# Field-pair tower on TensorE: sums of products in array tiles of 128 rows by 32 columns

## The reference

```python
z = jnp.sum(x, axis=-1)
xi = x[:, II, :]
xj = x[:, JJ, :]
outer = jnp.einsum('bpd,pde,bpe->bp', xi, kernels, xj)
h = jnp.concatenate([z, outer, dense_ctx], axis=1)
h = jnp.maximum(h @ W_top1 + b_top1, 0.0)      # 544 -> 512
h = jnp.maximum(h @ W_top2 + b_top2, 0.0)      # 512 -> 256
y = h @ W_top3                                 # 256 -> 1
```

## Time and profile before

| | |
|---|---|
| median of the runs | 843.35 us (843.25 to 846.5) |
| the profiled execution | 841.05 us, span 839.2 us |
| TensorE matmul (PE) | 804.7 us busy, 96% |
| VectorE (DVE) | 616.2 us, 73% |
| GpSimd (POOL), issuing gathers | 484.0 us, 58% |
| ScalarE (ACT) | 142.4 us, 17% |
| granted TensorE clock | 1.000 |

### The profile page before, as it was taken

One profiled execution on the slowest core, in us unless ns is written; L12 is line 12 of the kernel. 1 busy time (PEld: TensorE's weight loads), 2 busy tenths in 40 slices (PEclk: granted clock), 3 DMA queues, 4 the chain that ended last, 5 costly groups with the idle time before them and its releaser, 6 DMA issues.

```text
span 839.2 us, 33255 instructions
## 1 busy us (share of the span) xinstructions
PE 804.7 (96%) x15452; PEld 367.9 (44%) x15452; DVE 616.2 (73%) x613; ACT 142.4 (17%) x219; POOL 484.0 (58%) x518
## 2 busy tenths in 40 slices
PE   0699999999999999999999999999999999999998
PEld 0267767677754433333333333333333333333333
DVE  0477886588867788889855678988854588988850
ACT  0211022212120320120210320021111212011002
POOL 6777777777777777777777567767743340000000
PEclk9999999999999999999999999999999999999999
DMA  9611111111111111111111111111100010000000
GB/s 327 211 31 31 31 31 30 29 32 34 30 29 28 29 29 29 31 29 29 29 27 27 22 26 28 29 28 28 29 17 14 14 20 2 2 2 2 2 3 0
DMA packets 24387, 29.44 MB, mean 35 GB/s; under 512 B 13365, under 2 KB 13623, under 8 KB 24122
## 3 DMA queue, kind: packets, MB, share of 16 engines
q0 software_dynamic: 16384, 16.81, 10.2%
q1 hardware_dynamic: 7856, 10.49, 3.7%
q10 hardware_dynamic: 10, 0.01, 0.0%
HBM read 27.27 MB, written 0.01 MB: 33 GB/s over the span
## 4 chain that ended last, share of the span: by engine, by line
PE 93%; POOL 2%; DVE 2%; issue 1%; DMA 1%; ACT 0%; DVEq 0%; ACTq 0%
PE y L618 52%; PE accs L636 25%; PE y L598 4%; PE y L680 4%; PE y L668 3%; PE y L697 3%; POOL rows L371 2%; DVE prod L563 2%; PE y L673 1%; PE y L710 1%; DMA rows<-tbl,ids_sb 1%; PE y L649 0%; DMA ids_sb<-ids 0%; DVEq L265 0%; ACT h L484 0%
## 5 line engine op out<-in xcount | busy, mean ns | idle before, releaser
L563 DVE TENSOR_TENSOR prod<-y,xt 128x1024 f32<-128x1024 f32 (+1 forms) x525 | 576.4, 1157 | 170.9 <-PE y L618 167.5
L371 POOL DMA_INDIRECT rows<-tbl,ids_sb x512 | 483.3, 944 | 201.8 <-issue 125.1
L618 PE MATMUL y<-xt,kw 64*32 64x512 f32 (+1 forms) x9920 | 471.2, 509 | 5.6 <-DVE prod L563 2.2
L618 PEld LDWEIGHTS y<-xt,kw 64*32 64x32 f32 x9920 | 185.6, 107 | 245.3 <-issue 218.6
L636 PE MATMUL accs<-prod,ones_strip 64*32 64x512 f32 (+1 forms) x4960 | 242.6, 504 | 1.1 <-issue 0.6
L636 PEld LDWEIGHTS accs<-prod,ones_strip 64*32 64x32 f32 x4960 | 106.4, 107 | 110.3 <-issue 102.6
L417 ACT COPY xt<-y 128x1024 f32<-128x1024 f32 (+2 forms) x48 | 34.9, 728 | 381.8 <-PE y L598 381.8
L598 PE MATMUL y<-ident,rows 128*128 128x128 f32 x256 | 39.7, 289 | 24.8 <-DMA rows<-tbl,ids_sb 24.8
L535 DVE TENSOR_REDUCE z_rows<-rows 128x8 f32<-128x512 f32 (+1 forms) x80 | 42.9, 568 | 20.8 <-DMA rows<-tbl,ids_sb 20.8
L598 PEld LDWEIGHTS y<-ident,rows 128*128 128x128 f32 x256 | 27.6, 143 | 53.9 <-issue 39.6
L448 ACT COPY h_in<-accs 128x1024 f32<-128x1024 f32 (+1 forms) x10 | 8.4, 841 | 144.0 <-PE accs L636 144.0
(11 more groups left out here) (22 smaller groups left out, 61.9 us busy)
## 6 DMA issues: line engine op xcount, KB each, us to landing
rows<-tbl,ids_sb POOLq DMA_INDIRECT x512
kw<-pair_k SPq DMA_DIRECT2D x14, 512.0 KB, 10.2
w_sb<-w SPq DMA_DIRECT2D x1, 1024.0 KB
w_sb<-w SPq DMA_DIRECT2D x1, 512.0 KB
kw<-pair_k SPq DMA_DIRECT2D x1, 384.0 KB, 16.5
kw<-pair_k SPq DMA_DIRECT2D x1, 256.0 KB, 3.8
w1z_sb<-w1z SPq DMA_DIRECT2D x1, 256.0 KB
ids_sb<-ids SPq DMA_DIRECT2D x1, 224.0 KB, 2.6
```

Of the source, the lines that this page charges most:

```text
L371: pool.indirect_dma_start(out=rows[:, s, c, h, :], out_offset=None, in_=tables[f], in_offset=bass.IndirectOffsetOnAxis(ap=ids_sb[:, b, f:f ...
L563: nc.vector.tensor_tensor(prod_part(t, d, n), y_part(t, d, n), x, ALU.mult).then_inc(y_read, n)
L618: last = nc.tensor.matmul(y[columns, h, :], kw[part, d, columns], xt[part, slot_of(t, units[h][0] // 2), 0:w], start=True, stop=True)
```

## The change

The steps stay as they are: 8 matmuls of 64 rows by 32 columns. (The function that chose this by the width is replaced with the constant `STEP_COLUMNS` = 32, which is what it gave for all five tiles.) A sum is now one matmul for each unit over all 128 partitions, with 32 columns: `ones_strip` has ones in column 30 for partitions 0 to 63 and in column 31 for partitions 64 to 127, so that one matmul puts the two targets into rows 2s and 2s + 1 of the quadrant. Half as many units fit into an accumulator of 128 rows: `STRIPS` is 16, `CHUNK_STEPS` 32, `CHUNKS` 4. The accumulators are two banks that take turns, so the first sum of a chunk waits for the copy of the chunk before the last one. `h_in` and `w1_sb` lose their target index, and the rows of the first layer's weights are put in the new order on the host. The size of `w1` stays.

```diff
-STRIPS = 32
+STRIPS = 16
@@ constants, operands
-        h_in = sb("h_in", [P, CHUNKS, 2, TILE])
+        h_in = sb("h_in", [P, CHUNKS, TILE])
-        w1_sb = sb("w1_sb", [P, CHUNKS, 2, N1])
+        w1_sb = sb("w1_sb", [P, CHUNKS, N1])
-        ones_strip = sb("ones_strip", [P, 63])
+        ones_strip = sb("ones_strip", [P, 62])
-        accs = bank("accs", [P, 2, TILE])
+        accs = [bank(f"acc{i}", [P, TILE]) for i in range(2)]
@@ read_acc
-                nc.scalar.copy(h_in[:, c, :, 0:w], accs[:, :, 0:w]).then_inc(acc_read, 1)
+                nc.scalar.copy(h_in[:, c, 0:w], accs[(CHUNKS * t + c) % 2][:, 0:w]).then_inc(acc_read, 1)
@@ vector engine, at the start
-            dve.memset(ones_strip[:, STRIPS - 1:STRIPS], 1.0).then_inc(consts_made, 1)
+            dve.memset(ones_strip[0:DIM, 30:31], 1.0).then_inc(consts_made, 1)
+            dve.memset(ones_strip[DIM:P, 31:32], 1.0).then_inc(consts_made, 1)
@@ sum_group
-                if first % CHUNK_STEPS == 0 and c >= 1:
+                if first % CHUNK_STEPS == 0 and c >= 2:
-                    pe.wait_ge(acc_read, c)
+                    pe.wait_ge(acc_read, c - 1)
                 pe.wait_ge(y_read, N_STEPS * t + end)
                 for u in range(2 * first, 2 * end):
                     q, s = unit_place(u)
-                    for n in range(2):
-                        part = slice(DIM * n, DIM * n + DIM)
-                        last = nc.tensor.matmul(accs[32 * q:32 * q + 32, n, 0:w],
-                                                ones_strip[part, STRIPS - 1 - s:2 * STRIPS - 1 - s],
-                                                prod_part(t, u // 2)[part, u % 2, :], start=s == 0,
-                                                stop=ends_chunk(t, g) and u >= 2 * end - QUADRANTS)
+                    last = nc.tensor.matmul(acc[32 * q:32 * q + 32, 0:w], ones_strip[:, 30 - 2 * s:62 - 2 * s],
+                                            prod_part(t, u // 2)[:, u % 2, :],
+                                            start=s == 0, stop=ends_chunk(t, g) and u >= 2 * end - QUADRANTS)
                 last.then_inc(summed, 1)
@@ mlp1
                     for c in range(CHUNKS - 1):
-                        for n in range(2):
-                            nc.tensor.matmul(y[:, h, 0:w], w1_sb[:, c, n, j * P:(j + 1) * P], h_in[:, c, n, 0:w],
-                                             start=c == 0 and n == 0, stop=False)
+                        nc.tensor.matmul(y[:, h, 0:w], w1_sb[:, c, j * P:(j + 1) * P], h_in[:, c, 0:w],
+                                         start=c == 0, stop=False)
@@ mlp1, last chunk
-                    for n in range(2):
-                        last = nc.tensor.matmul(y[:, h, 0:w], w1_sb[:, CHUNKS - 1, n, j * P:(j + 1) * P],
-                                                h_in[:, CHUNKS - 1, n, 0:w], start=False, stop=n == 1)
+                    last = nc.tensor.matmul(y[:, h, 0:w], w1_sb[:, CHUNKS - 1, j * P:(j + 1) * P],
+                                            h_in[:, CHUNKS - 1, 0:w], start=False, stop=True)
```

More of the change, by code:

```diff
@@ L19 @@
 PROD_SLOTS = 8
-SPLIT_WIDTH = 256
+STEP_COLUMNS = 32
 SETS = COUPLES // 4
 QUADRANTS = 4
-STRIPS = 32
+STRIPS = 16
 J1, J2 = N1 // P, N2 // P
@@ L58 @@
 UNITS = 2 * N_STEPS
+CHUNKS = -(-N_STEPS // (2 * STRIPS))
 CHUNK_STEPS = 2 * STRIPS
-CHUNKS = -(-N_STEPS // CHUNK_STEPS)
 PAIRS = FIELDS * (FIELDS - 1) // 2
@@ L78, in pack @@
     return TILE // WIDTHS[t]
-def step_columns(t):
-    return 32 if WIDTHS[t] >= SPLIT_WIDTH else P
 def groups(t):
@@ L612, in do_step @@
                 w = WIDTHS[t]
-                size = step_columns(t)
-                for first in range(0, P, size):
-                    columns = slice(first, first + size)
+                for first in range(0, P, STEP_COLUMNS):
+                    columns = slice(first, first + STEP_COLUMNS)
                     for h in range(2):
@@ L625, in sum_group @@
                 c = CHUNKS * t + first // CHUNK_STEPS
+                acc = accs[c % 2]
                 w = WIDTHS[t]
-                if first % CHUNK_STEPS == 0 and c >= 1:
-                    pe.wait_ge(acc_read, c)
+                if first % CHUNK_STEPS == 0 and c >= 2:
+                    pe.wait_ge(acc_read, c - 1)
                 pe.wait_ge(y_read, N_STEPS * t + end)
@@ L712, in mlp3 @@
                 last.then_inc(y_full, 1)
-            pe.wait_ge(consts_made, 2)
+            pe.wait_ge(consts_made, 3)
             for what, t, n in PLAN:
@@ L757 @@
     k = np.zeros((P, N_STEPS, P), pair_k.dtype)
-    w1 = np.zeros((CHUNKS, 2, P, N1), w_top1.dtype)
+    w1 = np.zeros((CHUNKS, P, N1), w_top1.dtype)
     for d, step in enumerate(STEPS):
@@ L765 @@
                 k[DIM * h:DIM * h + DIM, d, DIM * n:DIM * n + DIM] = pair_k[pair] if i < f else pair_k[pair].T
-                w1[u // (QUADRANTS * STRIPS), n, 32 * q + s] = w_top1[FIELDS + pair]
+                w1[u // (QUADRANTS * STRIPS), 32 * q + 2 * s + n] = w_top1[FIELDS + pair]
     w1z = np.zeros((P, N1), w_top1.dtype)
@@ L776 @@
         dram_in("pair_k", k.reshape(P, N_STEPS * P)),
-        dram_in("w1", w1.transpose(2, 0, 1, 3)),
+        dram_in("w1", w1.transpose(1, 0, 2)),
         dram_in("w1z", w1z),
```

## The result

The changed kernel takes 867.16 us (median of 4 runs, 866.79 to 867.21) against 843.45 before: a ratio of 1.0274, 95% interval 1.0253 to 1.0295. The forecast was 869 in 853 to 884. The profiled execution took 866.79 us (span 865.0), 25.7 more than the one before.

The account below looks back on a forecast made before the run. TensorE (PE), busy 96% of the span, was taken as the bound. Profiled 841.05 us + 30.5 of seams - 4.2 hidden gave 867.4; the same +26.3 on the median gave 869.7; forecast 869 us, range 853 to 884.

Parts of the forecast that it names:

- The sums themselves, gain 0 and loss 0: Sum matmuls on PE: instructions halve, 4960 to 2480, but rounds and array time stay, 1.71 us for 4 steps.
- Rival 3: Sums: the four column tiles don't run side by side, +640 us, some 1500 us; chance 3%.
- Entries at 0.16 and 0.18 us: Shape change from steps to sums, 64x32 to 128x32: 92 at 512 columns, 32 at 256, 20.5 us together.
- Exits to steps at 0.135: Shape change from sums back to steps, 128x32 to 64x32: 82 times 0.135 us, 11.1 us.
- Exits to other work, -1.1: Sums to transposes or an mlp stage: seam already there, stagger shrinks by 0.027 us, 42 times, -1.1 us.
- the sum: Total over PE: 30.5 us of added seams less 4.2 hidden, +26.3 us on the profiled 841.05, giving 867.4.
- Hidden, 4.2: Added time absorbed by PE's waits: 4 us in the 256-column stages, 0.2 at the end of the last tile.
- The upper bound of 6: Most that PE's waits for VectorE in the 256-column stages could hide, in us; bounds 0 and 6.
- The allowance for that: Median before 2.3 us above the profiled run: same +26.3 gives 869.7, so 869 was taken between 867.4 and 869.7.
- Rival 1: Sums: loads of 128-row tiles don't overlap matmuls of the same rows, +15 to +65 us, about 905; chance 8%.
- Rival 2: Entries and exits between steps and sums: no seam between shapes sharing 32 columns, about 842, or 835; chance 10%.
- The rest at nothing: New mlp1 order, twenty h_in copies, two accumulators, w1 and one more memset: counted at no gain or loss.

Follow-up runs that it names:

- after_g2: The changed kernel with groups of sums of two slots instead of four; 892.94 us, ratio 1.0572 to the kernel before.
- the probe: Kernel before, sums still 64 by 32, plus one zero-weight matmul of 128 rows by 32 columns in each group of sums; 878.79 us, ratio 1.0399.
- narrow_g2: Kernel before with groups of two slots instead of four in the two 256-column tiles only; 834.94 us, ratio 0.989.
- best_g1: Kernel before with transposes moved to mlp pieces, field sums to transposes, groups of one slot in 256-column tiles, two elsewhere; 847.44 us, ratio 1.0039.
- best_g2: Kernel before with transposes moved to mlp pieces, field sums to transposes, and groups of two slots everywhere; 839.07 us, ratio 0.9936.

## Why the prediction was right, point by point

- *The sums themselves, gain 0 and loss 0*: right. The 2480 instructions go in rounds of four. Behind the first round of a block the median from one to the next is 0.429 us at 512 columns and 0.216 at 256, as before. Rival 3 is out.
- *Entries at 0.16 and 0.18 us, 20.5 us in all*: right. Measured 18.2 for the gaps and 3.0 for the first rounds behind them (0.024 each), 21.2.
- *Exits to steps at 0.135, 11.1 us*: right. Measured 9.3 and some 2.1 for the first rounds (0.026 each), 11.4.
- *Exits to other work, -1.1*: 38 to the 128 by 128 shape cost 4.3 us in place of 5.7, -1.4 (0.114 for 0.144 at 512 columns, and more at 256, where the old stagger was longer); the 4 to mlp3 lost their whole seam, -0.6, which I had not seen. Entries and exits together are 30.6 us, for 30.5 in the sum. The excess of the first terms and that of this one cancel, and that much is luck. The seams of the table grew by 29.4: the rest, -1.2, is in places that the sum doesn't have, in part the 21 exits from steps to transposes in the 256-column tiles (most 0.137 us, where many were 0.168).
- *Hidden, 4.2*: the waits fell by 4.1 us (4.7 with the other split), and 3.7 of it is in the 256-column tiles, where waits between rounds went from 10.3 to 6.7. So the place was right. The upper bound of 6 was drawn too low: it was read from idle time, which hides part of each wait, and there were 10 us to take. In after_g2 8.8 us more are gone and 0.2 is left in those tiles, but groups of two slots alone took 6.6 from the kernel before, so this run doesn't show what seams can hide. That 4 of the 10 were taken follows from no row; the size is in part luck.
- The sum said +26.3 us between profiled executions; it was 25.7. The forecast of 869 lies 1.8 above the median, because the median of the changed kernel is close to its profiled run, where that of before was 2.3 above. The allowance for that was the mis-sized term.
- *Rival 1* (loads not beneath matmuls of the same rows): out by the loads at 627.82 and 628.25. Its lower end, 0.02 us for each of 620 rounds, is 12 us and not the 15 of its sum. *Rival 2* (no seam between shapes that share 32 columns): out by the 0.147 and 0.113 us of the table, and by the probe. What carried the forecast was that the rows of 128 by 1 next to 64 by 32 were not a neighbour of the new pair but the pair itself: after the change the array goes from 128 by 32 to 128 by 1 without a seam, so for the array they are one shape. The Trainium skill (TensorEngine Tiling (Array Packing), Available Configurations) lists 128x32, 64x32 and 128x128 as different configurations. The seams of 0.113 to 0.147 and 0.114 us between them bear that out.
- *The rest at nothing*: nothing waits for the twenty copies (L443) in the trace after, and the rounds of 128 by 128 at 512 columns stand 1.2 us above their own time in all in both traces, so the new order in mlp1 cost nothing; the second accumulator was tried by itself and moved nothing.

What stays open: how the 0.09 us that is left of a seam without its stagger is made up, since no run takes it apart; and how much of a given wait a seam hides.

## What to carry to other kernels

When an engine's timeline is back to back, price a new tiling by the distance between starts of whole rounds, not by instruction counts or durations: half the matmuls over twice the rows is the same array time. Count how often the array's shape changes (rows and columns of the tile, not the operands' widths): here each change cost 0.11 to 0.15 us plus the weights that could not be loaded ahead (0.024). The 206 more of them cost 27.5 us in gaps and 5 in weights, 23.7 us net, though half of the sums' instructions were gone. Where two engines wait for each other by turns, shorter runs of each kind of work can win time back (9 us here), and a piece of work that looks movable may be what hides a transfer.

## What the runs showed of the hardware

- The seam does not depend on which side is small: 64x32 to 128x32 and to 128x128 mostly cost 0.137 and 0.138 us from round to round in the 512-column tiles, any shape of 128 rows to 64x32 0.093 to 0.094 from the last start. Rows alone (128x128 to 64x128, 0.093) or columns alone (128x32 to 128x128, 0.114 from round to round) are enough.
- For the array a matmul of 128 rows with 1 column of weights has the shape of one with 32: at the four changes from 128x32 to 128x1 the gap was 0 or 1 ns.
- A block of sums may be neither too near to its products nor too far from them: from 8 steps down to 4 at 256 columns gained 9 us (narrow_g2), from 4 to 2 lost 8 (best_g1 against best_g2).
